# A GNN layer and an attention layer: SyncE fetches a chunk of every 7th block row by row, and ScalarE makes the node-side one-hot from broadcast rows

## The chip, the core and the metric

The kernel runs on one core of one Trainium2 chip. The metric is the device time of one execution in microseconds, median over several runs. The engines are TensorE (PE; PEld is its weight load), VectorE (DVE), ScalarE (ACT), GpSimd (POOL) and SyncE (SP). SyncE computes nothing here: it issues DMAs and waits on semaphores.

## The reference, cut to what matters

There are 12500 nodes with 128 features and 200000 edges sorted by `dst`. Layer normalisation and relu stand ahead of each of two layers; each layer's result is added to its input.

```python
h = relu(layernorm(x))
# layer 0: message passing, mlp(h) = silu(h @ W1 + b1) @ W2 + b2
msgs = mlp_msg(concat[mlp_node(h)[dst], mlp_node(h)[src], mlp_edge(edge_attr)])    # 200000 x 64
agg = segment_sum(msgs, dst) / max(count(dst), 1)
out = h + mlp_upd(concat[h, agg]);  x = x + layernorm(out) * ln_g + ln_b
# layer 1: graph attention, 4 heads of 32, with self loops
h = relu(layernorm(x)) @ W
e = leaky_relu(a_src[src] + a_dst[dst], 0.2)
p = exp(e - segment_max(e, dst)[dst])
out = segment_sum(h[src] * p / segment_sum(p, dst)[dst], dst)
return x + out + bias
```

## The kernel before, in words

**Tiling.** The edges form 196 blocks (`NB`) of 1024, each of 8 chunks (`C`) of 128 edges. The nodes form 98 windows (`W`) of 128. As the edges are sorted, a walk through (block, window) pairs takes 294 steps (`NS`), two to a row of the loop, 147 rows. `build_steps` in the message pass works out the step table on the chip: which block and window each step has, and (`blockend`) after which step a block is done with.

**Stages.** The opening (`opening`) does the layer normalisation and the node MLP and stores the source-side table `Btab`, 64 floats a node. Each of its weights comes by a load of its own (half of them issued by ScalarE, line 364), and VectorE folds small weights together ahead of the first group (lines 424 to 432). The message pass walks all steps; from row 100 on, its rows also carry the update phase (`update_mean` and so on), which makes the new x and the table `Htab`, 136 floats a node. The attention pass walks all steps again and gathers from `Htab`. Between two stages all engines meet at a barrier (line 832).

**Gathers.** GpSimd does little but gather: `gather_blocks` (line 529) issues one indirect DMA for each chunk, 128 rows by 128 indices (line 541), into the slot of its block; there are 7 slots (`SLOTS`), `p_rows` in the message pass and `a_G` in the attention pass. Ahead of a block it waits for that block's index list (`src`) and for the last step that uses the block whose slot it takes (`p_z`).

**Row fetches.** In every 14th block (`SPAN`) GpSimd leaves out the last chunk. SyncE fetches its 128 rows one by one over the 12 blocks before (class `Rows`): `load` brings the 128 node numbers, `batch` reads 12 or 8 of them into registers (line 580) and issues as many DMAs of one row (line 584) into a spare tile `p_single` or `a_single`, and `place` (line 597) copies the spare into the slot when the steps are done with it.

**SyncE's loop.** `feed_messages` (line 708) goes through the blocks in one order. For each it waits until edge attributes can be overwritten (`s_s1`), loads the edge attributes of the block 6 ahead (line 718), waits for its gathers (line 746), announces it (`s_ready`), loads the index list of the block that takes this slot next (line 714), and does its share of the row fetches. `feed_blocks` (line 621) is the same for the attention pass, with broadcast flag rows in place of edge attributes (line 1422). VectorE waits for `s_ready` in each step before it adds the gathered rows (line 1056).

**One-hots.** Each step needs two one-hot matrices between its 1024 edges and the 128 nodes of its window. VectorE makes one in bf16 with edges on the partitions: `dst` less the window's first node (`p_rel`, line 1078), compared with a ramp in PSUM (`p_Sb`, line 1089). ScalarE casts it to f32 as `p_S` (line 1227), the stationary side of the segment sum (line 1365). TensorE transposes its 8 chunks (line 1318) and ScalarE copies the result out of PSUM as `p_ST` (line 1206), nodes on the partitions, for the expansion of the target-side table (line 1346). Engines run each row's work in program order; semaphores count steps.

Of the kernel before, what the change touches and what calls it, by code (L numbers as in the profile page):

```python
# [21 lines left out]
I32 = mybir.dt.int32  # L22
ACT = mybir.ActivationFunctionType
AX = mybir.AxisListType

P = 128
# [6 lines left out]
C = 8  # L33
# [6 lines left out]
BATCH = (12, 12, 12, 8, 12, 8, 12, 8, 12, 8, 12, 12)  # L40
# [23 lines left out]
assert W == NG * GW and NG % 2 == 0 and NS % 2 == 0 and NB % SPAN == 0 and sum(BATCH) == P and len(BATCH) < SPAN  # L64
# [32 lines left out]
def build(nc, t, out):  # L97

    main = ExitStack()
    with main:  # L100
# [3 lines left out]
        x1keep = nc.dram_tensor("x1keep", [NP, D], F32, kind="Internal").ap()  # L104
        flagrows = nc.dram_tensor("flagrows", [NB, P], F32, kind="Internal").ap()

# [12 lines left out]
        for name, shape, dt in [  # L119
# [10 lines left out]
            ("xr", [P, W], F32), ("xs", [P, W], F32), ("flag", [P, NB], F32),  # L130
            ("nv", [P, WX, 3, 2 * NH], BF16), ("attn", [P, WX, 2 * NH], F32),
# [8 lines left out]

        k["at"] = sb("at", [1, P], I32)
        k["singles"] = [sem("at"), [sem(f"row{n}") for n in range(3)], sem("to")]
        k["slots"] = [[sem(f"{n}{u}") for u in range(SLOTS)] for n in ("src", "rows", "side")]

        k["idx"] = [sb(f"idx{u}", [P, C], I32) for u in range(SLOTS)]

        with ExitStack() as ctx:
            opening(nc, t, k, hTkeep, Btab, lambda *a: sb(*a, ctx=ctx), sem, ctx)
        with ExitStack() as ctx:
            message_pass(nc, t, k, Btab, Htab, hTkeep, x1keep, flagrows, lambda *a: sb(*a, ctx=ctx), sem, ctx)  # L150
        with ExitStack() as ctx:
            attention_pass(nc, t, k, Htab, flagrows, x1keep, out, lambda *a: sb(*a, ctx=ctx), sem, ctx)
# [61 lines left out]
def opening(nc, t, k, hTkeep, Btab, sb, sem, ctx):  # L214
# [13 lines left out]
    iota_i = sb("iota_i", [P, P * C], I32)  # L228
# [4 lines left out]
    s1 = sb("n_s1", [H, GW * P])  # L233
    psT, psU, psV = (ctx.enter_context(nc.psum_tensor(f"n_ps{n}", [P, 2, 512], F32)) for n in "TUV")
# [3 lines left out]
    s_w, s_wc, s_id, s_v, s_pe, s_zero = (sem(f"c_{n}") for n in ("w", "wc", "id", "v", "pe", "zero"))  # L238
# [23 lines left out]
    with nc.Block() as block:  # L262
        @block.sync
        def _(sp):
# [28 lines left out]
            run_pairs(sp, body, NG, 3)  # L293
            sp.wait_ge(s_wc, 32)
# [5 lines left out]
        def _(pool):  # L300
            pool.iota(iota_i[:, :], [[1, P], [0, C]], base=0, channel_multiplier=0).then_inc(s_id, 1)
            pool.memset(k["ident"][:, :], 0.0).then_inc(s_id, 1)
            pool.wait_ge(s_id, 2)
# [9 lines left out]
        def _(pe):  # L313
            pe.wait_ge(s_id, 3)
# [79 lines left out]
        def _(dve):  # L394
# [6 lines left out]
            def fold():  # L401
# [27 lines left out]
                dve.wait_ge(s_id, 3)  # L429
                dve.tensor_copy(k["iota_nc"][:, :, :].rearrange("p n c -> p (n c)"), iota_i[:, :]).then_inc(s_v, 1)  # L430
                dve.wait_ge(s_v, link())
                dve.tensor_copy(k["identb"][:, :], k["ident"][:, :]).then_inc(s_v, 1)
# [96 lines left out]
def gather_blocks(nc, pool, table, rows, idx, s_used, s_turn, k, turns, s_table=None):  # L529
# [3 lines left out]
    def block(i, odd, u, used):  # L533
        if due(16 * (i + 1 + turns)):
            pool.wait_ge(s_idx[u], 16 * (i + 1 + turns))
        if used is not None:
            if due(used):
                pool.wait_ge(s_used, used)
            pool.sem_inc(s_turn, 1)
        for c in range(C - 1 if odd and u == SLOTS - 1 else C):  # L540
            pool.indirect_dma_start(  # L541
                out=rows[:, u * C + c, :], out_offset=None, in_=table,
                in_offset=bass.IndirectOffsetOnAxis(ap=idx[u][:, c:c + 1], axis=0)).then_inc(s_g[u], 16)
# [5 lines left out]
    for u in range(SLOTS):  # L549
        block(0, False, u, None)  # L550
# [3 lines left out]
    for u in range(SLOTS):  # L554
        block(1, True, u, used[u])
    with pool.Fori(1, NB // SPAN) as r:
        used = used_by(r * SPAN, SPAN)
        for odd in range(2):
            for u in range(SLOTS):
                block(2 * r + odd, odd == 1, u, used[odd * SLOTS + u])  # L560


class Rows:


    def __init__(self, nc, sp, t, k, table, spare, at, to, s_used, s_turn, turn):
        self.nc, self.sp, self.t, self.k, self.table, self.spare, self.at, self.to = nc, sp, t, k, table, spare, at, to
        self.s_used, self.s_turn, self.turn = s_used, s_turn, turn
        self.s_at, self.s_row, self.s_to = k["singles"]
        self.total = NB // SPAN * turn  # L570

    def load(self, r):
        self.sp.dma_start(self.at[:, :], self.t["single"][bass.ds(r, 1), :]).then_inc(self.s_at, 16)

    def batch(self, r, n):
        sp, first = self.sp, sum(BATCH[:n])
        if n == 0:
            sp.wait_ge(self.s_at, 16 * (r + 1 + self.total))
            sp.sem_inc(self.s_turn, 1)
        which = self.nc.values_load_multi_w_load_instructions(  # L580
            self.at[0:1, first:first + BATCH[n]], engines=[sp.engine], min_val=0, max_val=NP - 1,
            skip_runtime_bounds_check_because="indices of nodes")[1]
# [4 lines left out]
    def place(self, r):  # L587
        sp = self.sp
        used = self.nc.values_load_multi_w_load_instructions(
            self.k["blockend"][0:1, 0, bass.ds(r * SPAN + SPAN - 1, 1)], engines=[sp.engine], min_val=0, max_val=NS,  # L590
            skip_runtime_bounds_check_because=BOUNDED)[1][0]
        for n in range(3):
            sp.wait_ge(self.s_row[n], 16 * sum(BATCH[n::3]) * (r + 1 + self.total))
            sp.sem_inc(self.s_turn, 1)
        sp.wait_ge(self.s_used, used)
        sp.sem_inc(self.s_turn, 1)
        sp.dma_start(self.to, self.spare[:, :]).then_inc(self.s_to, 16)

    def placed(self, r):
        self.sp.wait_ge(self.s_to, 16 * (r + 1 + self.total))  # L600
        self.sp.sem_inc(self.s_turn, 1)


def gathers(r, odd, u, turns):

    if u < SLOTS - 1:
        return 16 * C * (2 * r + odd + 1 + turns)
    return 16 * (2 * C - 1) * (r + turns // 2) + 16 * (2 * C - 1 if odd else C)


def step_singles(singles, r, n, final):

    if n < len(BATCH):
        singles.batch(r, n)
    elif n == SPAN - 2:
        singles.place(r)
    elif n == SPAN - 1 and not final:
        singles.load(r + 1)


def feed_blocks(nc, sp, t, idx, s_used, s_turn, s_ready, k, side, turns, then, singles):


    s_idx, s_g, s_side = k["slots"]

    def load_idx(b, u):
        sp.dma_start(idx[u][:, :], t["src"].rearrange("(b p) c -> b p c", p=P)[bass.ds(b, 1)]
                     .rearrange("o p c -> (o p) c")).then_inc(s_idx[u], 16)

    def arrived(r, odd, u):  # L630
        i = 2 * r + odd
        sp.wait_ge(s_g[u], gathers(r, odd, u, turns))
        sp.sem_inc(s_turn, 1)
        if due(16 * (i + 1 + turns)):
            sp.wait_ge(s_side[u], 16 * (i + 1 + turns))
# [4 lines left out]
    singles.load(0)  # L640
    then()
    def blocks(r, odd, first=False, final=False):
        i = 2 * r + odd
        used = used_at(i)
        for u in range(SLOTS):
            if odd and u == SLOTS - 1:
                singles.placed(r)
            arrived(r, odd, u)
            if not final:
# [1226 lines left out]
```

## Time and profile before

| | |
|---|---|
| median of 3 runs | 4092.73 us (4090.88 to 4094.87) |
| the profiled execution | 4091.22 us, span 4089.1 us, mean granted clock 0.838 |
| busy of the span | PE 83%, PEld 73%, DVE 62%, ACT 70%, POOL 73% |
| gathers | 1554 in each pass, 1471.4 us busy in the message pass, 1470.8 in the attention pass |
| first gather, message pass / attention pass | 112.13 us / 2109.75 us |

How to read the rows further down: times are microseconds from the span's start, a mean is in ns. A row names line, engine, operation, and out<-in by the program's names, without buffer numbers. "SPq" and "POOLq" are the queues in which SyncE and GpSimd issue. "issue" is time in which an engine waited for nothing that the profile shows. The share of busy time is an average over stages with different limits; the views by stage say more.

### The profile page before, as it was taken

To read this page: it belongs to the slowest core of one execution; us is meant where nothing else is said; L and a number is where in the kernel's file an instruction comes from. 1 tells how busy PE (TensorE), PEld (TensorE's weight loads), DVE (VectorE), ACT (ScalarE), POOL (GpSimd) and SP (SyncE) were. 2 spreads that over 40 slices of the span, in tenths; PEclk is the share of its full clock that TensorE was granted. 3 is DMA by queue.
4 is the path that set the end of the run, shared out by engine and by line. 5 is a ranking of instruction groups with operands and counts; after the bars stand their busy time and mean duration, and the time that the engine had idled before them with its cause. 6 is when DMAs were issued, how large, how long until landed. Compare 5 with 4: busy or idle time off the path is not lost. (4 is left out here: it accounts for less than half of the span.)

```text
span 4089.1 us, 126775 instructions
## 1 busy us (share of the span) xinstructions
PE 3382.9 (83%) x30848; PEld 2976.2 (73%) x30849; DVE 2517.0 (62%) x10511; ACT 2850.5 (70%) x5940; POOL 2965.8 (73%) x3134
## 2 busy tenths in 40 slices
PE   7789888999988899999947777777777778777777
PEld 4677777777777788888847777777777767766776
DVE  5752222222222256777748777777777777888888
ACT  6466565656556577788738777777777777877777
POOL 2677777777777777777737777777777777777774
PEclk8789999999899899999967777777777777777777
DMA  5322222222222233333342222222222222332332
GB/s 159 88 60 53 54 55 53 56 53 53 55 54 53 60 83 91 91 96 95 81 120 58 57 58 58 57 58 58 58 57 58 58 58 63 79 78 76 78 78 58
DMA packets 319769, 282.90 MB, mean 69 GB/s; under 512 B 143418, under 2 KB 242924, under 8 KB 319532
## 3 DMA queue, kind: packets, MB, share of 16 engines
q0 software_dynamic: 99456, 159.33, 15.9%
q1 hardware_dynamic: 139224, 79.62, 7.4%
q10 hardware_dynamic: 80852, 41.75, 3.5%
q14 instruction: 205, 1.68, 0.1%
q8 instruction: 32, 0.52, 0.1%
HBM read 249.58 MB, written 29.40 MB: 68 GB/s over the span
## 5 line engine op out<-in xcount | busy, mean ns | idle before, releaser
L541 POOL DMA_INDIRECT a_G<-Htab,idx x1554 | 1470.8, 946 | 526.3 <-issue 464.0
L541 POOL DMA_INDIRECT p_rows<-Btab,idx x1554 | 1471.4, 947 | 475.1 <-issue 473.4
L1799 PE MATMUL a_psA<-a_GP,a_S 128*128 128x132 f32 x4704 | 892.5, 365 | 2.7 <-DVE a_GP L1634 2.7
L1799 PEld LDWEIGHTS a_psA<-a_GP,a_S 128*128 128x128 f32 x4704 | 821.5, 268 | 8.2 <-DVE a_GP L1634 3.1
L1056 DVE TENSOR_TENSOR p_z<-p_psZ,p_rows 128x512 f32<-128x512 f32 x294 | 195.9, 689 | 829.4 <-SPq L746 679.6
L1206 ACT COPY p_ST<-p_psT 128x1024 bf16<-128x1024 bf16 x294 | 300.5, 1022 | 563.7 <-PE p_psT L1318 543.4
L1730 ACT CAST a_S<-a_Sb 128x512 f32<-128x512 bf16 x588 | 608.6, 1144 | 0.0
L1365 PE MATMUL p_psA<-p_msg,p_S 128*128 128x65 f32 x4704 | 589.9, 284 | 10.9 <-ACT p_S L1227 9.8
L1365 PEld LDWEIGHTS p_psA<-p_msg,p_S 128*128 128x128 f32 x4704 | 571.6, 201 | 16.5 <-issue 12.8
L1227 ACT CAST p_S<-p_Sb 128x1024 f32 (+1 forms) x294 | 582.6, 1982 | 0.0
L1341 PEld LDWEIGHTS p_psZ<-wc,p_s 128*128 128x128 f32 x2352 | 325.1, 206 | 204.7 <-issue 103.5
L1341 PE MATMUL p_psZ<-wc,p_s 128*128 128x128 f32 x2352 | 339.3, 291 | 80.0 <-DVE p_z L1056 80.0
L1324 PE MATMUL p_psH<-arena,ew 128*128 x588 | 350.3, 680 | 24.1 <-issue 0.2
L1634 DVE TENSOR_TENSOR a_GP<-a_G,a_ep 128x1056 f32<-128x1056 f32 x294 | 366.8, 1248 | 0.0
L1688 ACT COPY a_ST<-a_psT 128x1024 bf16<-128x1024 bf16 x294 | 302.6, 1029 | 45.0 <-issue 27.4
L1318 PE MATMUL p_psT<-identb,p_Sb 128*128 128x128 bf16 x2352 | 292.8, 260 | 44.3 <-issue 25.1
L1318 PEld LDWEIGHTS p_psT<-identb,p_Sb 128*128 (+1 forms) x2352 | 255.6, 147 | 82.5 <-issue 62.5
L1705 ACT ACTIVATE arena<-arena,a_f x1176 | 282.3, 311 | 7.1 <-DVE arena L1516 1.7
L1789 PE MATMUL a_psCD<-ident,a_csh 4*128 4x4 f32 x588 | 140.6, 307 | 158.6 <-DVE a_csh L1522 157.1
L1789 PEld LDWEIGHTS a_psCD<-ident,a_csh 4*128 4x128 f32 x588 | 114.8, 242 | 207.2 <-DVE a_csh L1522 202.9
L1346 PE MATMUL p_psZ<-arena,p_ST 128*128 x7056 | 264.4, 196 | 0.0
L1346 PEld LDWEIGHTS p_psZ<-arena,p_ST 128*128 128x128 bf16 x7056 | 258.1, 100 | 4.7
(212 smaller groups left out, 5165.8 us busy)
## 6 DMA issues: line engine op xcount, KB each, us to landing
arena<-in_ea SPq DMA_DIRECT2D x196, 256.0 KB
p_single<-Btab SPq DMA_DIRECT2D x1792, 0.2 KB
a_single<-Htab SPq DMA_DIRECT2D x1792, 0.5 KB
p_rows<-Btab,idx POOLq DMA_INDIRECT x1554
a_G<-Htab,idx POOLq DMA_INDIRECT x1554
Htab<-u_H ACTq DMA_DIRECT2D x49, 136.0 KB
arena<-Htab SPq DMA_DIRECT2D x7, 952.0 KB
n_x<-in_x SPq DMA_DIRECT2D x14, 448.0 KB, 4.0
```

The lines of the kernel that those rows point to most:

```text
L541: pool.indirect_dma_start(out=rows[:, u * C + c, :], out_offset=None, in_=table, in_offset=bass.IndirectOffsetOnAxis(ap=idx[u][:, c:c + 1] ...
L1206: act.copy(ST[u][:, :, :], psT[:, :, :]).then_inc(s_ST, 1)
L1227: act.copy(S32[v][:, :, :].rearrange("p c n -> p n c"), onehot(row - 3 + u, v)).then_inc(s_S32, 1)
L1318: m = pe.transpose(psT[:, c, :], hot[:, :, c], k["identb"][:, :])
L1324: pe.matmul(psH[:, :], k["ew1"][:, :], ea[:, bass.ds(slot, 1), :].rearrange("p o e -> p (o e)"), start=True, stop=True).then_inc(s_H, 1)
L1341: pe.matmul(psZ[v][:, 2 * e:2 * e + 2, :], s1[v][:, e * P:(e + 1) * P], k["wc2"][:, :], start=e == 0, stop=False)
L1346: m = pe.matmul(psZ[v][:, c, :], ST[v][:, c, :], a, start=False, stop=part == 2 and c == C - 1)
L1365: m = pe.matmul(psA[v], S32[v][:, c, :], msg[v][:, c, :], start=c == 0, stop=c == C - 1)
L1634: dve.tensor_tensor(GP[u][:, :, :].rearrange("p c (h f) -> p c h f", h=NH), G[:, slot2, 0:HR].rearrange("p c (h f) -> p c h f", h=NH), bc( ...
L1688: act.copy(ST[v][:, :, :], psT[:, :, :]).then_inc(s["ST"], 1)
L1730: m = act.copy(S32[v][:, cs, :].rearrange("p c n -> p n c"), Sb[v][:, :, cs])
L1799: m = pe.matmul(psA[v][:, 0:HR], S32[v][:, c, :], GP[v][:, c, :], start=c == 0, stop=c == C - 1)
```

## The change

**Row fetches.** The row-wise chunk is now that of every 7th block: the last chunk of the last block in each round of 7, save in the first round, so 27 rounds a pass instead of 14. SyncE spreads the 128 rows over 7 blocks (19, 18, 18, 18, 18, 18, 19). The node numbers are multiplied by the row's size once, in the opening, and stored in DRAM (`offsets`); `batch` reads byte offsets and addresses the table as a flat array of bytes. The spare and the offsets are double-buffered. One index list holds a whole round, 128x56, and is loaded once in 7 blocks.

**One-hots of the message pass.** For each block SyncE loads one more thing, `load_near`: the block's 1024 targets modulo 128, in bf16, one row of DRAM (`lowrows`, made in the opening) broadcast to 128 partitions. ScalarE makes `p_ST` from it in two passes, `Abs` of the row less the partition's number and `Relu` of one less that. The transposes, their PSUM tile and the copy go. VectorE writes the f32 one-hot `S32` itself, one instruction from the ramp in PSUM, `wnode` and `dst`; the bf16 one-hot and ScalarE's cast go. `psH` has two buffers.

**The opening** loads `nodes` and `ends` (the targets as 98 rows), masks and casts the latter to `low`, multiplies the former twice, and SyncE stores `offsets` and `lowrows` at its end, with a wait for each.

```diff
-BATCH = (12, 12, 12, 8, 12, 8, 12, 8, 12, 8, 12, 12)
+BATCH = (19, 18, 18, 18, 18, 18, 19)
...
             run_pairs(sp, body, NG, 3)
+            sp.wait_ge(s_off, 18)
+            for n in range(2):
+                sp.dma_start(offsets[n], bytes_[n][:, :]).then_inc(s_off, 16)
+            sp.wait_ge(s_off, 50)
+            sp.wait_ge(s_low, 18)
+            sp.dma_start(lowrows.rearrange("(q r) e -> q (r e)", r=2), low[:, :]).then_inc(s_low, 16)
+            sp.wait_ge(s_low, 34)
...
             for to, src in loads[1::2]:
                 act.dma_start(to, src).then_inc(s_w, 16)
+            act.dma_start(nodes[:, :], t["single"]).then_inc(s_off, 16)
+            act.dma_start(ends[:, :], t["dstrow"].rearrange("(q r) e -> q (r e)", r=2)).then_inc(s_low, 16)
...
+                dve.tensor_scalar(k["back"][:, :], row_i[:, :], -1.0, None, ALU.mult).then_inc(s_v, 1)
...
+                dve.tensor_scalar(ends[:, :], ends[:, :], P - 1, None, ALU.bitwise_and).then_inc(s_low, 1)
+                dve.wait_ge(s_low, 17)
+                dve.tensor_copy(low[:, :], ends[:, :]).then_inc(s_low, 1)
...
-    def block(i, odd, u, used):
-        if due(16 * (i + 1 + turns)):
-            pool.wait_ge(s_idx[u], 16 * (i + 1 + turns))
+    def block(r, odd, u, used, whole=False):
+        if u == 0:
+            pool.wait_ge(s_idx[odd], 16 * (r + 1 + turns // 2))
...
-        for c in range(C - 1 if odd and u == SLOTS - 1 else C):
+        for c in range(C if whole or u < SLOTS - 1 else C - 1):
...
-        which = self.nc.values_load_multi_w_load_instructions(
-            self.at[0:1, first:first + BATCH[n]], engines=[sp.engine], min_val=0, max_val=NP - 1,
+        at = self.nc.values_load_multi_w_load_instructions(
+            self.k["at"][0:1, odd * P + first:odd * P + first + BATCH[n]], engines=[sp.engine], min_val=0,
...
-            sp.dma_start(self.spare[first + p:first + p + 1, :], self.table[bass.ds(which[p], 1), :]
-                         ).then_inc(self.s_row[n % 3], 16)
+            sp.dma_start(self.spare[first + p:first + p + 1, odd, :].bitcast(U8),
+                         self.table[bass.ds(at[p], self.size)].unsqueeze(0)).then_inc(self.s_row[n % 4], 16)
...
+    def step(self, i, odd, u, first, final):
+        if not first and u == 0:
+            self.landed(i)
+        if not first and u == SLOTS - 2:
+            self.place(i, odd)
+        if not final:
+            self.batch(i + 1, 1 - odd, u)
+            if u == 0 and not (isinstance(i, int) and i + 2 >= ROUNDS):
+                self.load(i + 2, odd)
...
+    def load_near(b, u):
+        sp.dma_start(near[:, u, :], lowrows[bass.ds(b, 1), :].rearrange("o e -> (o e)").partition_broadcast(P)
+                     ).then_inc(s_ea[u], 16)
...
+                        dve.scalar_tensor_tensor(
+                            S32[v][:, :, :], bc(psI[:, :], 1, C), k["wnode"][:, bass.ds(j, 1)],
+                            bc(k["dstf"][:, bass.ds(blk[u], 1), :].rearrange("p o c -> p (o c)"), 2, P),
+                            ALU.subtract, ALU.is_equal).then_inc(s_S32, 1)
...
-                        act.copy(ST[u][:, :, :], psT[:, :, :]).then_inc(s_ST, 1)
+                        act.activation(ST[u][:, :, :].rearrange("p c n -> p (c n)"), dist[:, :], ACT.Relu,
+                                       scale=-1.0, bias=k["one"][:, :]).then_inc(s_ST, 1)
...
-                        act.copy(S32[v][:, :, :].rearrange("p c n -> p n c"), onehot(row - 3 + u, v)).then_inc(s_S32, 1)
...
-                        for c in range(C):
-                            m = pe.transpose(psT[:, c, :], hot[:, :, c], k["identb"][:, :])
-                        m.then_inc(s_T, 1)
```

On SyncE, in the message pass, one block of the loop stood like this (line 584 goes on in the same pairs for 12 or 8 rows):

```order
L718 DMA arena<-in_ea 128x512
L714 DMA idx0<-in_src 128x8
L580 TENSOR_LOAD at
L584 ISA
L584 DMA p_single<-Btab 1x64
L584 ISA
L584 DMA p_single<-Btab 1x64
```

Now one block stands like this:

```order
L749 DMA arena<-in_ea 128x512
L752 DMA p_S32<-lowrows 128x1024
L612 TENSOR_LOAD at
L616 DMA p_single<-Btab 1x256 x18
```

The instruction ahead of each row (the register work that the profile records as FUSED_REGOPS) and the index list of each block are gone; the broadcast rows (`p_S32` is the tile of which `near` is a part) are new.

On GpSimd, the message pass, where the second round ends and the loop begins, with the semaphores waited for, before:

```order
L541 DMA p_rows<-Btab,idx5 128x64 [waits src5,p_z]
L541 DMA p_rows<-Btab,idx5 128x64 x7
L541 DMA p_rows<-Btab,idx6 128x64 [waits src6,p_z]
L541 DMA p_rows<-Btab,idx6 128x64 x6
...
L541 DMA p_rows<-Btab,idx0 128x64 [waits src0,p_z]
```

The last two blocks of a loop's first round and the first of its second, now:

```order
L571 DMA p_rows<-Btab,idx0 128x64 [waits p_z]
L571 DMA p_rows<-Btab,idx0 128x64 x7
L571 DMA p_rows<-Btab,idx0 128x64 [waits p_z]
L571 DMA p_rows<-Btab,idx0 128x64 x6
L571 DMA p_rows<-Btab,idx1 128x64 [waits src1,p_z]
L571 DMA p_rows<-Btab,idx1 128x64 x7
```

The wait for an index list stands once in 7 blocks instead of at each, and every round's last block has 7 gathers where every second one had.

On SyncE, from the opening's last store to the message pass, before:

```order
L283 DMA Btab<-n_b1 128x7x64
L262 UNCONDITIONAL_BRANCH
L833 UNCONDITIONAL_BRANCH
L714 DMA idx0<-in_src 128x8
```

And now:

```order
L291 DMA Btab<-n_b1 128x7x64
L304 DMA offsets<-bytes0 28x128
L304 DMA offsets<-bytes1 28x128
L307 DMA lowrows<-low 98x2048
L270 UNCONDITIONAL_BRANCH
L868 UNCONDITIONAL_BRANCH
L657 DMA idx0<-in_src 128x56
```

Three stores moved in between the table's last rows and the end of the stage, and one index list of 56 columns stands where seven of 8 stood.

## Rows read from the trace of the kernel before

**Rows 1.** The page's part 4: the chain that ended last, by engine, by line.
```profile
POOL 27%; issue 11%; DVE 4%; PE 3%; DMA 1%; DVEq 1%; POOLq 1%; ACT 0%; SPq 0%; ACTq 0%
POOL a_G L541 27%; PE a_psA L1799 2%; DMA a_G<-Htab,idx 1%; DVE a_GP L1634 1%; POOLq L546 0%; DVE a_csh L1522 0%; DVE arena L1516 0%; DVEq L1409 0%; PE a_psCD L1789 0%; PE a_psCD L1834 0%; DVE nv L83 0%; DVE a_e L1527 0%; DVE a_loc L1461 0%; DVE a_nq L1554 0%; DVE a_eq L1539 0%
```

**Rows 2.** The page's part 5: count | busy us, mean ns | idle before, its releaser.
```profile
L541 POOL DMA_INDIRECT a_G<-Htab,idx x1554 | 1470.8, 946 | 526.3 <-issue 464.0
L541 POOL DMA_INDIRECT p_rows<-Btab,idx x1554 | 1471.4, 947 | 475.1 <-issue 473.4
```

**Rows 3.** Timeline of GpSimd: start, length, instruction, [idle before]; first, last, first gather.
```profile
112.13 1.17 POOL L541 DMA_INDIRECT p_rows<-Btab,idx  x1 [1.66 <-DMA idx<-in_src]
...
2056.02 0.94 POOL L541 DMA_INDIRECT p_rows<-Btab,idx  x1 [0.30 <-issue]
...
2109.75 0.94 POOL L541 DMA_INDIRECT a_G<-Htab,idx  x1 [52.79 <-POOLq L832]
```

**Rows 4.** Timelines of SyncE, VectorE and GpSimd: block 60 and its slot's refill.
```profile
720.00 0.36 SPq L714 DMA_DIRECT2D idx<-in_src  x1
720.20 1.29 DVE L1056 TENSOR_TENSOR p_z<-p_psZ,p_rows 128x512 f32<-128x512 f32 x2 [5.32 <-SPq L746]
778.59 0.94 POOL L541 DMA_INDIRECT p_rows<-Btab,idx  x1 [0.30 <-issue]
```

**Rows 5.** What SyncE's queue waited for: total us, times, longest.
```profile
SPq L746 <- DMA p_rows<-Btab,idx: 644.2, 194, 7.0
SPq L633 <- DMA a_G<-Htab,idx: 569.9, 168, 6.9
```

**Rows 6.** Timelines of ScalarE, VectorE and SyncE: the opening, and two stage starts.
```profile
8.47 0.55 ACTq L364 DMA_DIRECT2D attd<-in_att_dst  x1
...
20.84 0.69 DVE L430 CAST iota_nc<-iota_i 128x1024 bf16<-128x1024 int32 x1
...
102.12 5.08 SPq L283 DMA_DIRECT2D Btab<-n_b  x2
109.76 3.50 SPq L714 DMA_DIRECT2D idx<-in_src  x7
...
2109.08 2.32 SPq L1422 DMA_DIRECT2D a_frow<-flagrows  x7
```

**Rows 7.** Timeline of SyncE: two blocks of the message pass.
```profile
700.36 0.36 SPq L714 DMA_DIRECT2D idx<-in_src  x1
701.86 4.83 SPq L584 DMA_DIRECT2D p_single<-Btab  x12
...
710.46 0.36 SPq L714 DMA_DIRECT2D idx<-in_src  x1
711.76 3.19 SPq L584 DMA_DIRECT2D p_single<-Btab  x8
```

**Rows 8.** Instructions of line 584: count, ns min/median/max, first and last start.
```profile
L584 SPq FUSED_REGOPS  x3584: 37/37/47, 126.7 to 4042.8; - x200
L584 SPq MOVE p_single<-Btab x1792: 29/29/38, 126.8 to 2045.6; - x200
L584 SPq DMA_DIRECT2D p_single<-Btab x1792: 224/228/308, 126.9 to 2045.7; - x200
```

**Rows 9.** Windows: us, busy of PE, PEld, DVE, ACT, POOL, PEclk, DMA share, GB/s.
```profile
1600.00:1800.00 200.00, 194.65 (x1967) 165.05 (x1963) 139.61 (x564) 158.91 (x267) 151.20 (x161) 0.99 0.36 95
2200.00:2600.00 400.00, 306.64 (x2608) 283.42 (x2606) 311.28 (x1452) 302.82 (x850) 302.44 (x321) 0.74 0.23 58
```

**Rows 10.** The message pass's wide groups; the last from 300 to 1300 us alone.
```profile
L1056 DVE TENSOR_TENSOR p_z<-p_psZ,p_rows 128x512 f32<-128x512 f32 x294 | 195.9, 689 | 829.4 <-SPq L746 679.6
L1206 ACT COPY p_ST<-p_psT 128x1024 bf16<-128x1024 bf16 x294 | 300.5, 1022 | 563.7 <-PE p_psT L1318 543.4
L1227 ACT CAST p_S<-p_Sb 128x1024 f32 (+1 forms) x294 | 582.6, 1982 | 0.0
L1318 PE MATMUL p_psT<-identb,p_Sb 128*128 128x128 bf16 x2352 | 292.8, 260 | 44.3 <-issue 25.1
...
L1089 DVE TENSOR_TENSOR p_Sb<-p_psI,p_rel 128x1024 bf16 x151 | 97.3, 686 | 7.0 <-DVE p_rel L1078 3.0
```

More of the change, by code:

```diff
@@ L22 @@
 I32 = mybir.dt.int32
+U8 = mybir.dt.uint8
 ACT = mybir.ActivationFunctionType
@@ L130, in build @@
             ("xr", [P, W], F32), ("xs", [P, W], F32), ("flag", [P, NB], F32),
+            ("back", [P, 1], F32), ("one", [P, 1], F32),
             ("nv", [P, WX, 3, 2 * NH], BF16), ("attn", [P, WX, 2 * NH], F32),
@@ L554, in gather_blocks @@
     for u in range(SLOTS):
-        block(1, True, u, used[u])
-    with pool.Fori(1, NB // SPAN) as r:
+        block(0, 1, u, used[u])
+    with pool.Fori(1, ROUNDS // 2) as r:
         used = used_by(r * SPAN, SPAN)
@@ L569, in __init__, with load, batch @@
         self.s_at, self.s_row, self.s_to = k["singles"]
[L570 to L575, printed above, removed]
+        self.before = (ROUNDS - 1) * turn
+    def load(self, i, odd):
+        self.sp.dma_start(self.k["at"][0:1, odd * P:(odd + 1) * P], self.offsets[bass.ds(i, 1), :]).then_inc(self.s_at, 16)
+    def batch(self, i, odd, n):
         sp, first = self.sp, sum(BATCH[:n])
@@ L601, in placed @@
+    def placed(self, i):
+        self.sp.wait_ge(self.s_to, 16 * (i + self.before))
         self.sp.sem_inc(self.s_turn, 1)
-def gathers(r, odd, u, turns):
-    if u < SLOTS - 1:
[L607 to L618, printed above, removed]
@@ L621, in feed_blocks, with landed @@
[L621 to L632, printed above, removed]
+    def landed(self, i):
+        for n in range(4):
+            self.sp.wait_ge(self.s_row[n], 16 * sum(BATCH[n::4]) * (i + self.before))
+            self.sp.sem_inc(self.s_turn, 1)
@@ L639, in feed_blocks @@
         side(u, u)
-    singles.load(0)
+    singles.load(1, 1)
     then()
@@ L655, in blocks @@
                 side(i * SLOTS + u + 2, (u + 2) % SLOTS)
-            step_singles(singles, r, odd * SLOTS + u, final)
+            singles.step(i, odd, u, first, final)
     def used_at(i):
@@ L739, in blocks @@
                 load_ea(i * SLOTS + u + SLOTS - 1, ahead)
+                load_near(i * SLOTS + u + SLOTS - 1, ahead)
             if not (final and u > 1):
-                sp.wait_ge(s_ea[landing], 16 * (i + 1 + (u > 1)))
+                sp.wait_ge(s_ea[landing], 32 * (i + 1 + (u > 1)))
                 sp.sem_inc(s_eardy, 1)
-            if odd and u == SLOTS - 1:
-                singles.placed(r)
-            sp.wait_ge(s_g[u], gathers(r, odd, u, 0))
+            if u == SLOTS - 1 and not first:
+                singles.placed(i)
+            sp.wait_ge(s_g[u], gathers(i, u, 0))
             sp.sem_inc(s_ready, 1)
-            load_idx(u if final else (i + 1) * SLOTS + u, u)
-            step_singles(singles, r, odd * SLOTS + u, final)
+            if u == 0:
+                load_idx(sp, t, k, 0 if final else i + 1, 1 - odd)
+            singles.step(i, odd, u, first, final)
     def used_at(i):
@@ L1302, in body @@
                     m.then_inc(s_ft, 1)
+                if isinstance(row, int) and 1 <= row <= NG:
+                    pe.wait_ge(s_piece, PIECE * row)
                 if isinstance(row, int) and row == HIDE:
```

215 lines of the change are left out of this document (112 added, 103 removed).

## Prediction

> **What bounds the kernel now.** I read the chain that ended last first, then the two costliest groups. The chain is one long run of GpSimd gathers with "issue" between them [rows 1]. Each pass has 1554 of them, 0.947 us busy and 0.304 us of issue apiece [rows 2]: (1471.4 + 473.4) / 1554 = 1.251 us from one gather to the next. Nearly all idle time before them is "issue", so GpSimd waits for nobody: in the message pass 473.4 of 475.1 us. The two passes are 2 x 1945 of 4089 us; what is left is the opening (first gather at 112.13), the 53 us between the last gather of pass one and the first of pass two [rows 3], and a tail of a few steps. Whatever the change does to VectorE, ScalarE and TensorE counts only if one of them, or SyncE, becomes slower than the gathers.
>
> How far is that? In the message pass SyncE announces block 60 just ahead of its next index list at 720.00, VectorE adds the rows at 720.20, and GpSimd refills that slot at 778.59 [rows 4]: the consumers could be over 50 us later before a gather waits. SyncE is the engine to watch. It idles on landing gathers for 644.2 us of the message pass and 569.9 us of the attention pass [rows 5], which is 46.0 and 40.7 us in each stretch of 14 blocks, 111 x 1.251 = 138.9 us long.
>
> **1. Fewer gathers: a gain.** Before, GpSimd drops one gather in 14 blocks; now it drops one in 7, except in the first round: 56 + 27 x 55 = 1541 instead of 1554. That is 13 x 1.251 = 16.3 us a pass, -32.5 us in both, as long as GpSimd stays the bound. One wait per block on the index list becomes one per 7 blocks; that is worth nothing, since the wait doesn't show between gathers.
>
> **2. The opening: a loss.** ScalarE issues two more loads (0.55 us each [rows 6]) ahead of its first activation, which the first group waits for: +1.1. VectorE's fold gets a mask over 98x2048 int32, a cast of that to bf16 and four small operations. The nearest row is a 128x1024 int32 to bf16 cast of 0.69 us [rows 6]; so the cast is 1.4, the mask 1.4 to 2.8 (I take 2.0), the small ones 4 x 0.25: +4.4. The groups behind run as a dependent chain, so I let both shift the end. Then SyncE, before it closes the opening, stores the offsets, waits, stores the masked rows, waits. Now it goes from the end of its last issue (102.12 + 5.08 = 107.20) to the next stage at 109.76 [rows 6], 2.56 us with one landing in it. Two stores in sequence are two such landings with some 1.5 us of issues, and the old wait lies under the first: +4.0. Sum **+9.5 us**, bounds +5 (mask cheap, part of the chain slack) and +14.
>
> **3. SyncE's work: the term that decides.** In 14 blocks of the message pass it is busy 138.9 - 46.0 = 92.9 us now. Per 14 blocks the change does this:
> - Rows: 256 instead of 128. Now one costs (4.83 - 3.19) / 4 = 0.41 us [rows 7]: FUSED_REGOPS 37, MOVE 29 and the DMA 228 ns [rows 8], so 0.116 us of gaps, 0.039 each. The new row has its byte offset ready, and the register instruction is gone from the order above: 0.41 - 0.037 - 0.039 = 0.334. Ends: 0.30 (the remaining instructions with one gap) and 0.41 (nothing saved). Back-to-back issues without any register instruction between them took 2.32 / 7 = 0.33 [rows 6], so it can't be much less; I take 0.34, as the first rows of a batch are longer. 256 x 0.34 - 128 x 0.41 = +34.6.
> - Register loads: between an index issue's end and the first row lie 1.14 us for 12 values and 0.94 for 8 [rows 7], 0.05 per value, so 1.45 for 18: 14 x 1.45 - 12.9 = +7.4.
> - Index lists: 12 of 14 issues go (0.36 and two register instructions, 0.5): -6.0.
> - The broadcast rows: one more 128-partition issue per block, 0.55: +7.7.
> - A second set of waits, list load and placing store: +2.
>
> Sum 92.9 + 45.7 = **138.6 us against 110 x 1.251 = 137.6 for the gathers**. This is a tie. SyncE would fall behind by 1.0 us in 14 blocks, 13 us over the 13.5 stretches in which it fetches rows, and it starts some 4 us later, since the first broadcast rows wait for the step table. The last round has no rows to fetch, so SyncE catches up there; the steps (10.5 in it, at 6.55 us) catch up only as far as engines allow. TensorE is busy 194.65 of 200 us late in the pass [rows 9], 6.4 us a step, and loses 1.0 us of transposes [rows 10]: at about 5.5 us a step 10 us are made up. Of a 17 us backlog 7 are left; I take **+5**, ends 0 and 75 (below).
> In the attention pass the same changes without the broadcast rows give 138.9 - 40.7 + 38.0 = 136.2 against 137.6. GpSimd stays the bound there, by 1.4 us in 14 blocks: **0**.
>
> **4. The one-hots: nothing.** ScalarE loses the 1.98 us cast and the 1.02 us copy and gets two 128x1024 activations; the copy of that size is the nearest row [rows 10], so 2 x 1.02: -0.96 us a step. VectorE trades the 0.69 us bf16 one-hot for a 128x1024 f32 one; the nearest row is 128x512 f32 out of PSUM in 0.69 [rows 10], 1.4 at twice the size: about +0.7 a step, on an engine at 139.61 of 200 us [rows 9]. TensorE loses 8 transposes. All lie beside gathers with 50 us of slack. After the last gather ScalarE's casts go and VectorE's one-hots come in a few rows, -3 to +3.
>
> What VectorE does could reach GpSimd in one way. Late in the message pass, with VectorE at 70%, GpSimd is busy 151.20 of 200 us, and 302.44 of 400 in the attention pass with VectorE at 78% [rows 9]: the same 75.6%, so nothing on VectorE slows it today. The Trainium skill ("SBUF — State Buffer", Who interferes with whom) says that a VectorE instruction with two SBUF inputs, or in a two-port mode, keeps GpSimd out of a shared port, and that one with at most one SBUF input doesn't. The new one-hot takes its ramp from PSUM and its indices from SBUF; by the rule it costs nothing, as in my sum.
>
> **The sum.** 4091.2 (profiled execution, span 4089.1) - 32.5 + 9.5 + 5 = 4073.2. The median of the runs is 1.5 above that execution: **4075**.
>
> **Rivals.**
> - *SyncE becomes the bound of the message pass* (slower). If a row doesn't shrink as worked out, or an issue stretches when issues stand closer, each 0.01 us adds 2.6 us to 14 blocks, 35 us to the pass. The point: 4101 needs a backlog of about 41 us, (41 - 4) / 13.5 = 2.7 over the gathers, a row of 0.347. At 0.36: 143.7, 6.1 x 13.5 = 82 + 4 - 10 = 76, so about 4145; at the old 0.41 some 4315, and the attention pass would bind too. For it: the margin is zero. Against: the order has one instruction less in each row, and its time is in the rows.
> - *The gain of pass one is given back*: the same with a row of 0.341 to 0.347, a backlog of 24 to 40 us: 4084 to 4101, no measurable change.
> - *More gain*: SyncE stays ahead (row 0.33 or less) and the fold hides: -32.5 + 5, so 4060 to 4064.
> - *TensorE's clock* falls once the transposes are gone. It shows 0.99 with TensorE at 97% late in the message pass and 0.74 at 77% in the attention pass, between its two levels of 1.2 and 2.4 GHz [rows 9]. At 0.74, 5.4 us of steps would take 7.2, over the 6.55 of the gathers: 0.65 x 94 (the steps from row 100 on, where the update work runs) = 60, less what is absorbed, about 4120. But then TensorE would never idle, and the row with no idle time shows 0.99. The Trainium skill ("TensorE: Matmul & The Clock Gate", HAM oscillation) makes idle gaps the cause of the lower level; by that rule this rival limits itself.
> - *The port*: were GpSimd held for each new one-hot, 294 x 1.4 = up to 412 us, about 4485. Only the rows above speak, and they speak against it.
>
> **How the numbers follow.** A measurement of this kernel can tell about 0.2% (8.2 us) from no change: faster is under 4084.5, slower over 4100.9. Forecast, 4062 to 4084: 0.51. More gain: 0.06. Given back: 0.17. SyncE the bound: 0.20. Clock: 0.04. Port: 0.02. So faster 0.57, same 0.17, slower 0.26. Below 4062 I leave 0.06; above 4125 half of the SyncE case and the port, 0.12: the range is 4062 to 4125; the forecast's own is 4062 to 4084.
>
> **What the next profile shows.** 1541 gathers a pass, still 1.25 us apart, with "issue" before them. Row fetches 0.33 to 0.35 us apart without FUSED_REGOPS. SyncE's idle time on landing gathers nearly gone in the message pass (under 100 us, from 644) and some 20 to 60 us in the attention pass. First gather at about 121 instead of 112, first attention gather at 2102 or so, the end 20 us earlier. I am wrong if GpSimd waits on VectorE's sums in the message pass, if a row takes over 0.347 us, or if the opening grows by more than 14 us.

## The result: slower by 15%, and the profile after

The changed kernel takes 4721.77 us (median of 4 runs, 4715.08 to 4730.44) against 4091.81 before: a ratio of 1.154, 95% interval 1.152 to 1.156. The forecast was 4075, the range 4062 to 4125. The profiled execution has a span of 4719.1 us at a mean granted clock of 0.76 (0.838 before).

The page of the changed kernel, part 4, the chain that ended last, by engine and by line, against [rows 1]:

```profile
SPq 38%; issue 8%; DVE 1%; DVEq 0%; PE 0%; ACT 0%; ACTq 0%
SPq L616 19%; SPq L612 15%; SPq L1449 1%; SPq L694 1%; SPq L1454 0%; SPq L657 0%; SPq L626 0%; SPq L621 0%; PE a_psA L1826 0%; SPq L605 0%; DVEq L1436 0%; DVE arena L1543 0%; DVE a_csh L1549 0%; SPq L671 0%; SPq L668 0%
```

The chain is SyncE's. Line 616 is the row DMA; line 612 is the instruction that loads a list of byte offsets into SyncE's registers. GpSimd is no longer among the engines on the chain. The chain reaches back to the start of the attention pass; for the message pass the waits further down speak. Part 5 of the same page, the gathers against [rows 2], and VectorE's add of the gathered rows against [rows 10]:

```profile
L571 POOL DMA_INDIRECT a_G<-Htab,idx x1541 | 1458.6, 947 | 817.8 <-issue 461.5
L571 POOL DMA_INDIRECT p_rows<-Btab,idx x1541 | 1458.2, 946 | 811.8 <-issue 444.9
L1091 DVE TENSOR_TENSOR p_z<-p_psZ,p_rows 128x512 f32<-128x512 f32 x294 | 196.9, 688 | 1220.4 <-SPq L783 1112.8
```

13 gathers a pass are gone and one still takes 0.946 us, but GpSimd now idles 812 us before them where it idled 475. VectorE waits 1112.8 us for SyncE's announcement that a block is there (line 783), and GpSimd in turn for VectorE and, in the message pass, for index lists that SyncE loads late. The waits of GpSimd and of SyncE in the changed kernel (what was waited for: us in total, times, longest; line 867 is the barrier between stages), SyncE's against [rows 5]:

```profile
POOL p_rows L571 <- DVE p_z L1091: 302.5, 72, 13.0
POOL a_G L571 <- DVE a_GP L1661: 260.2, 117, 12.7
POOL a_G L571 <- POOLq L867: 96.1, 1, 96.1
...
POOL p_rows L571 <- DMA idx<-in_src: 64.4, 14, 9.0
...
SPq L668 <- DMA a_G<-Htab,idx: 5.7, 1, 5.7
...
SPq L783 <- DMA p_rows<-Btab,idx: 3.1, 1, 3.1
```

SyncE hardly waits for gathers any more: 3.1 us in the message pass, from 644.2, and 5.7 in the attention pass, from 569.9. The pace follows from the windows (us, busy of PE, PEld, DVE, ACT, POOL with counts, PEclk, DMA share, GB/s), one in the middle of each pass:

```profile
600.00:2000.00 1400.00, 997.16 (x9046) 840.38 (x9045) 468.67 (x1042) 650.32 (x861) 863.69 (x915) 0.81 0.27 74
2800.00:4400.00 1600.00, 1109.05 (x9056) 1027.52 (x9056) 1112.73 (x5189) 1051.60 (x2953) 1049.32 (x1111) 0.69 0.21 55
```

915 gathers in 1400 us make 110 x 1400 / 915 = 168.3 us for 14 blocks of the message pass, 1111 in 1600 us make 158.4 in the attention pass. GpSimd alone would need 137.6, and the prediction's sum for SyncE was 138.6 and 136.2.

Where the 630 us of the span went is read from the first and the last gather of each pass, against [rows 3]:

```profile
115.55 1.18 POOL L571 DMA_INDIRECT p_rows<-Btab,idx  x1 [2.02 <-DMA idx<-in_src]
...
2382.55 0.94 POOL L571 DMA_INDIRECT p_rows<-Btab,idx  x1 [0.30 <-issue]
...
2479.62 0.94 POOL L571 DMA_INDIRECT a_G<-Htab,idx  x1 [96.12 <-POOLq L867]
...
4658.95 0.94 POOL L571 DMA_INDIRECT a_G<-Htab,idx  x1 [0.30 <-issue]
```

The first gather comes at 115.55, 3.4 later; the message pass's gathers take 2268.0 us, 323 more; from the last of them to the first of the attention pass it is 96.1 us, 43 more; the attention pass's gathers take 2180.3, 236 more; the tail after the last gather is 24 longer, 59 us from 35.

### The profile page after: what moved, and what is told of

Its sections match the earlier page's. It is cut to its first block and busy times, and to the rows that moved or that the text cites. A ratio compares the mean times of both kernels' runs of the same rounds, so it can differ in the third digit from the quotient of the medians.

```text
span 4719.1 us, 122417 instructions
## 1 busy us (share of the span) xinstructions
PE 3338.5 (71%) x28496; PEld 2919.1 (62%) x28497; DVE 2625.8 (56%) x10223; ACT 2691.3 (57%) x5940; POOL 2940.4 (62%) x3109
## 5 line engine op out<-in xcount | busy, mean ns | idle before, releaser
L1091 DVE TENSOR_TENSOR p_z<-p_psZ,p_rows 128x512 f32<-128x512 f32 x294 | 196.9, 688 | 1220.4 <-SPq L783 1112.8
L1368 PEld LDWEIGHTS p_psZ<-wc,p_s 128*128 128x128 f32 x2352 | 378.5, 239 | 596.3 <-DVE p_z L1091 486.8
L1368 PE MATMUL p_psZ<-wc,p_s 128*128 128x128 f32 x2352 | 408.0, 329 | 441.3 <-DVE p_z L1091 441.1
L1245 ACT ACTIVATE p_s<-p_psH,eb 128x512 f32<-128x512 f32 x294 | 199.7, 679 | 467.3 <-PE p_psH L1351 467.2
L1241 ACT ACTIVATE p_ST<-p_dist,one 128x1024 bf16<-128x1024 bf16 x294 | 337.5, 1148 | 105.6 <-PE p_psZ L1373 90.8
L1260 ACT ACTIVATE p_msg<-p_z 128x512 f32<-128x512 f32 x294 | 185.8, 632 | 359.1 <-DVE p_z L1091 358.6
L1235 ACT ACTIVATE p_dist<-p_S,back 128x1024 bf16 x294 | 335.8, 1142 | 90.8 <-issue 57.4
L1861 PE MATMUL a_psCD<-ident,a_loc 128*4 128x128 f32 x294 | 95.2, 324 | 411.2 <-DVE a_loc L1488 363.2
L1698 ACT COPY a_ca<-a_G 128x32 f32 x294 | 72.7, 247 | 524.7 <-SPq L671 516.7
L1109 DVE SCALAR_TENSOR_TENSOR p_S<-p_psI,wnode,dstf 128x1024 f32<-128x1024 f32 x294 | 364.1, 1280 | 0.0
L1488 DVE TENSOR_TENSOR_SCAN a_loc<-scanmask,a_ca 128x32 f32<-128x32 f32 x294 | 66.4, 226 | 461.4 <-ACT a_ca L1698 451.2
```

The costliest lines, as they stand in the source:

```text
L1109: dve.scalar_tensor_tensor(S32[v][:, :, :], bc(psI[:, :], 1, C), k["wnode"][:, bass.ds(j, 1)], bc(k["dstf"][:, bass.ds(blk[u], 1), :].rear ...
L1235: act.activation(dist[:, :], near[:, bass.ds(blk1[u] % SLOTS, 1), :].rearrange("p o e -> p (o e)"), ACT.Abs, bias=k["back"][:, :]).then_in ...
L1241: act.activation(ST[u][:, :, :].rearrange("p c n -> p (c n)"), dist[:, :], ACT.Relu, scale=-1.0, bias=k["one"][:, :]).then_inc(s_ST, 1)
L1368: pe.matmul(psZ[v][:, 2 * e:2 * e + 2, :], s1[v][:, e * P:(e + 1) * P], k["wc2"][:, :], start=e == 0, stop=False)
```

## What SyncE does in a block

The timeline of SyncE in the changed kernel, two blocks of the message pass, against [rows 7] (start, length, instruction; line 657 is the index list, 616 the row fetches, 749 the edge attributes, 752 the broadcast rows):

```profile
708.76 0.33 SPq L657 DMA_DIRECT2D idx<-in_src  x1
711.45 6.58 SPq L616 DMA_DIRECT2D p_single<-Btab  x19
...
718.72 0.36 SPq L749 DMA_DIRECT2D arena<-in_ea  x1
719.27 0.36 SPq L752 DMA_DIRECT2D p_S<-lowrows  x1
723.75 5.79 SPq L616 DMA_DIRECT2D p_single<-Btab  x18
729.80 0.36 SPq L749 DMA_DIRECT2D arena<-in_ea  x1
```

The rows are what they were worked out to be: 5.79 / 18 = 0.32 us each, 0.33 on average over the pass. But from 719.63, the end of the broadcast load's issue, to 723.75 nothing is issued, 4.1 us, where the prediction had 1.45. The instructions of line 612, first the two of these blocks and then all of them (count, ns min/median/max, first and last start):

```profile
L612 SPq TENSOR_LOAD <-at x1: 1613/1613/1613, 709.7 to 709.7; - x1
...
L612 SPq TENSOR_LOAD <-at x1: 3844/3844/3844, 719.8 to 719.8; - x1
...
L612 SPq TENSOR_LOAD <-at x378: 1603/3852/4593, 134.6 to 4619.7; - x189
```

The first load of a round, 19 values, takes 1.61 us; the next, 18 values, 3.84. Over the seven loads of a round the medians in the message pass are 1.61, 3.85, 3.84, 3.85, 3.84, 3.71 and 4.04 us. The trace of the kernel before has such loads too, 8 or 12 values (line 580) and 7 values of the table of block ends (line 751):

```profile
L580 SPq TENSOR_LOAD <-at x336: 528/942/1292, 125.9 to 4037.1; - x168
...
L751 SPq TENSOR_LOAD <-blockend x28: 1108/1643/1918, 121.0 to 1996.2; - x28
```

Seven values took 1.64 us there where twelve took 0.94. The lists of line 580 start at 0, 12, 24, 36, 44 and so on, all multiples of 4; the changed kernel's at 0, 19, 37, 55, 73, 91, 109. The table of line 751 is the third row of 203 values in its tile, so its lists start at 406, 413, 420, 427 and so on. Every fourth of them starts at a multiple of 4, and these seven took 1.11 to 1.13 us, the 21 others at least 1.64. The third and the fourth:

```profile
L751 SPq TENSOR_LOAD <-blockend x1: 1120/1120/1120, 255.0 to 255.0; - x1
...
L751 SPq TENSOR_LOAD <-blockend x1: 1643/1643/1643, 331.0 to 331.0; - x1
```

## Experiments

**Theory A**: a load goes four values at a time where its list starts at a multiple of 4 values, and one by one elsewhere. **Theory B**: the loads are slow because of the row fetches in flight ahead of them. **Theory C**: they are slow because they are long.

**Batches of 20 and 16.** Every list starts at a multiple of 4.

```diff
-BATCH = (19, 18, 18, 18, 18, 18, 19)
+BATCH = (20, 20, 16, 20, 16, 20, 16)
```

> The changed kernel with batches of 20, 20, 16, 20, 16, 20, 16 rows, so that each list of register values starts at a multiple of 4 values. Theory A (SyncE's register load reads four values at a time only where its list starts at a multiple of 4 values, and one by one elsewhere, 0.21 us each): a load of 16 or 20 takes 1.1 to 1.5 us instead of 3.85, SyncE's work for 14 blocks falls from 168 to about 136 us, under the 137.6 of the gathers; GpSimd is the bound again, and the time is 4062 to 4080 us. Theory B (the loads are slow because they stand behind row fetches that are still in flight, the first of a round being fast because it follows a wait): loads after the first stay at 3.8 us or more, the time stays at about 4720. Theory C (a load of more than some 16 values is slow): the loads of 16 are fast, those of 20 are not, the time is about 4450.

Measured: 4079.23 us, a ratio of 0.9965 to the kernel before (0.9952 to 0.9977). All loads of line 612, and SyncE's waits:

```profile
L612 SPq TENSOR_LOAD <-at x378: 1131/1251/1904, 142.8 to 3975.7; - x189
...
SPq L668 <- DMA a_G<-Htab,idx: 170.7, 72, 9.9
SPq L783 <- DMA p_rows<-Btab,idx: 95.9, 26, 10.1
```

Another list of batch sizes takes 640 us off, and GpSimd is the bound again: its gathers take 1927.2 and 1930.2 us in the two passes, from 1944.8 and 1944.3 in the kernel before. Theories B and C fall: behind as many row fetches as before, loads of 16 take 1.13 us and loads of 20 take 1.36.

**Batches of 18.** Every other list starts at a multiple of 4, the others at a multiple of 2.

```diff
-BATCH = (19, 18, 18, 18, 18, 18, 19)
+BATCH = (18, 18, 18, 18, 18, 18, 20)
```

> The changed kernel with batches of 18, 18, 18, 18, 18, 18, 20 rows: the lists start at 0, 18, 36, 54, 72, 90, 108, so every other one is at a multiple of 4 values and the others at a multiple of 2 alone, with the same rows in flight ahead of each. Theory A: loads 3, 5 and 7 of a round take 1.4 to 1.6 us, loads 2, 4 and 6 either stay at 3.85 (four at a time needs a multiple of 4) or fall to about 2.3 (pairs); the time is then about 4350 or about 4150. Theory B: all six stay at 3.8, time about 4720.

Measured: 4323.04 us (one run). Three loads in a row, lists at 18, 36 and 54, all of 18 values behind 18 row fetches:

```profile
L612 SPq TENSOR_LOAD <-at x1: 3835/3835/3835, 897.9 to 897.9; - x1
...
L612 SPq TENSOR_LOAD <-at x1: 1561/1561/1561, 909.1 to 909.1; - x1
...
L612 SPq TENSOR_LOAD <-at x1: 3855/3855/3855, 918.4 to 918.4; - x1
```

The same count in the same surroundings takes 1.56 or 3.84 us by its start alone, and a multiple of 2 is no better than an odd start.

**The kernel before, its lists one value off.**

```diff
-BATCH = (12, 12, 12, 8, 12, 8, 12, 8, 12, 8, 12, 12)
+BATCH = (11, 12, 12, 8, 12, 8, 12, 8, 12, 8, 12, 13)
```

> The kernel before with batches of 11, 12, 12, 8, 12, 8, 12, 8, 12, 8, 12, 13: every list after the first starts one value short of a multiple of 4. Theory A: 12 values take 2.6 us instead of 0.94 and 8 take 1.7 instead of 0.72, 16 us more for SyncE in 14 blocks, which its 46 us of idle time take up: its waits on landing gathers fall from 644 to about 420 us in the message pass, and the time stays within 5 us of the kernel before. Theories B and C: the loads stay at 0.94 and 0.72, since their surroundings and counts are the same.

Measured: 4092.41 us, a ratio of 1.0009 (1.0000 to 1.0019). The loads of line 580, and SyncE's waits:

```profile
L580 SPq TENSOR_LOAD <-at x336: 1158/2662/3142, 122.6 to 4043.8; - x168
...
SPq L746 <- DMA p_rows<-Btab,idx: 395.4, 178, 7.2
SPq L633 <- DMA a_G<-Htab,idx: 315.2, 127, 6.9
```

Twelve values take 2.66 us and eight 1.86. SyncE loses some 250 us of idle time in each pass and the time doesn't move: the same price is free where SyncE has 46 us to spare in 14 blocks. From all loads of these kernels: off a multiple of 4, 1.86 us for 8 values, 2.66 for 12, 3.84 for 18 and 4.04 for 19, which is 0.20 us a value and some 0.25 at the start; at a multiple of 4, 0.72 for 8, 0.94 for 12, 1.13 for 16 and 1.36 for 20, which is some 0.21 for each four values. The Trainium skill ("Runtime: NRT & Kernel Launch", Instruction fetch mechanics) has about 200 ns a register even for loads in bulk; the runs, whose lists lie in SBUF, agree for lists off a multiple of 4 and differ for those on it.

**The two parts apart.** The row fetches alone are the kernel before with the changed `Rows`, `gather_blocks` and index lists, and batches of 20 and 16. Against the run with these batches:

```diff
-            sp.dma_start(lowrows.rearrange("(q r) e -> q (r e)", r=2), low[:, :]).then_inc(s_low, 16)
...
-                load_near(i * SLOTS + u + SLOTS - 1, ahead)
...
-                        dve.scalar_tensor_tensor(
-                            S32[v][:, :, :], bc(psI[:, :], 1, C), k["wnode"][:, bass.ds(j, 1)],
...
+                        dve.tensor_tensor(onehot(row, u), psI[:, :, :], bc(rel[u][:, :], 1, P),
+                                          ALU.is_equal).then_inc(s_S, 1)
...
+                            m = pe.transpose(psT[:, c, :], hot[:, :, c], k["identb"][:, :])
```

The one-hots alone are the kernel before with these same lines the other way round, the new one-hots in and the row fetches, index lists and opening stores of offsets as they were:

```diff
+                load_near(i * SLOTS + u + SLOTS - 1, ahead)
...
+                        dve.scalar_tensor_tensor(
+                            S32[v][:, :, :], bc(psI[:, :], 1, C), k["wnode"][:, bass.ds(j, 1)],
...
-                            m = pe.transpose(psT[:, c, :], hot[:, :, c], k["identb"][:, :])
```

> The row fetches alone: byte offsets, every 7th block, batches of 20 and 16 as in the run before, but the one-hots, the transposes and the opening's masks of the kernel before. Theory A (GpSimd binds both passes, so each gather left out is worth 1.25 us, and the new one-hots bring nothing but their cost: 8 us in the opening and about 7 us more between the last gather of the message pass and the first of the attention pass): 4092 - 32.5 + 4 for the offsets in the opening = 4063 us, with the stretch between the passes back at 53 us from 60.6 and SyncE's idle time on landing gathers in the message pass at about 200 us, 108 more than with the broadcast rows. Rival D (the one-hots carry part of the gain, by giving TensorE time): the time is 4079 us or more, and GpSimd waits for VectorE's sums in the update rows.

> The one-hots alone, with the row fetches of the kernel before (every 14th block, batches of 12 and 8). Theory A: 1554 gathers a pass at 1.251 us as before; the opening is some 8 us longer and the stretch between the passes about 7 us longer, so about 4105 us (4098 to 4112); SyncE's idle time on landing gathers in the message pass falls from 644 to about 530 us. Rival D: 4092 us or less.

In this comparison every kernel took 6700 to 6900 us, the kernel before too (6938.79), with VectorE and ScalarE waiting for what the profile calls remote (row fetches 6919.67, ratio 0.9971; one-hots 6692.39, ratio 0.9639). Why is open, and so is why the one-hots gained there. Both were run again. The expectation speaks of another chip; the record has the same number, 13, for both comparisons, and in the second the kernel before took 4091.89 us.

> The row fetches alone once more, on another chip: in the run above every kernel of the comparison, the kernel before too, took some 6900 us. Theory A as there: 4092 - 32.5 + 4 = 4063 us, the stretch between the passes at 53 us, SyncE's idle time on landing gathers in the message pass at about 200 us. Rival D: 4079 us or more.

> The one-hots alone once more, on another chip. Theory A as above: about 4105 us (4098 to 4112), 1554 gathers a pass 1.251 us apart, SyncE's idle time on landing gathers in the message pass at about 530 us. Rival D: 4092 us or less. On the chip of the run above the one-hots alone took 3.6% off all the same, where TensorE, VectorE and ScalarE waited for what the profile calls remote and GpSimd waited for VectorE; if the gain came from there being fewer instructions, nothing of it shows here.

Measured: the row fetches alone 4066.11 us, ratio 0.9936 (0.9922 to 0.9951); the one-hots alone 4095.05, ratio 1.0012 (1.0003 to 1.0020). SyncE's wait on gathers in the message pass and the first gather of the attention pass (in brackets GpSimd's idle time before it, the stretch between the passes), first of the row fetches, then of the one-hots:

```profile
SPq L762 <- DMA p_rows<-Btab,idx: 226.8, 94, 10.1
...
2105.26 0.94 POOL L557 DMA_INDIRECT a_G<-Htab,idx  x1 [61.11 <-POOLq L849]
```

```profile
SPq L769 <- DMA p_rows<-Btab,idx: 533.0, 174, 6.7
...
2114.86 0.94 POOL L557 DMA_INDIRECT a_G<-Htab,idx  x1 [53.62 <-POOLq L852]
```

The gain is the row fetches'; the one-hots alone cost about 3 us and 111 us of SyncE's idle time (644.2 to 533.0), 0.57 us a block, where the prediction gave the broadcast load 0.55. Two expectations fell. The longer stretch between the passes is there with the old one-hots (61.1 us) and not with the new ones alone (53.6, from 52.8). And the one-hots alone were expected at 4098 to 4112 and came out below that: the stretch did not grow by 7, and the first gather came 4.3 us later, not 8.

**Batches levelled.** Fewer rows in the block that has the index list and in the one that places.

```diff
-BATCH = (20, 20, 16, 20, 16, 20, 16)
+BATCH = (16, 20, 20, 20, 20, 16, 16)
```

> The row fetches alone with batches of 16, 20, 20, 20, 20, 16, 16: fewer rows in the block that also has the index list, the waits on landed rows and the table of block ends, and fewer where the spare is placed. With 20, 20, 16, 20, 16, 20, 16 SyncE announced the seven blocks of a round 3.7, 4.1, 3.0, 1.6, 1.6, 1.9, 3.2 us after their last gather, before 1.4 to 1.9. Theory E (the 7 to 8 us by which the stretch between the passes grew, 61 from 53, are these late announcements, which the update rows can't win back since TensorE is busy 97% there): the announcements come 2 us or less behind in most blocks, the stretch goes back to 53 to 56 us, and the time falls by about 5, to 4061. Rival F (the stretch is set by something else, as the kernel before with slower register loads showed 60 us there with announcements on time): it stays near 60 and the time at 4066.

> The whole change with batches of 16, 20, 20, 20, 20, 16, 16. With 20, 20, 16, 20, 16, 20, 16 the announcements came 6.7, 7.8, 7.1, 5.2, 4.5, 2.7, 5.0 us behind in the message pass. Theory E: 3 to 6 us behind, the stretch between the passes 2 to 4 us shorter than 60.6, the time 4074 to 4078. Rival F: no change of the stretch, 4079.

Measured: the row fetches alone 4064.68 us, ratio 0.9932 (0.9919 to 0.9946); the whole change 4067.48, ratio 0.9946 (0.9933 to 0.9960). These two and the row fetches above can't be told from one another; all three are 0.5 to 0.7% faster than the kernel before. The first gather of the attention pass, row fetches alone and whole change:

```profile
2102.04 0.94 POOL L557 DMA_INDIRECT a_G<-Htab,idx  x1 [63.46 <-POOLq L849]
```

```profile
2099.02 0.94 POOL L571 DMA_INDIRECT a_G<-Htab,idx  x1 [57.20 <-POOLq L867]
```

The announcements came 1.5 to 2.4 us (row fetches alone) and 2.0 to 3.5 us (whole change; medians by block of a round) behind the last gather, as levelling meant. With the row fetches alone the stretch stayed long all the same, as rival F has it; with the whole change it became 3 us shorter, as theory E has it. But its time fell by 12 us, below the 4074 to 4078 expected: of the 14.1 us between the two profiled spans 8.7 lie in the opening, whose first 100 us had a granted clock of 0.97 here and of 0.85 with batches of 20 and 16. The windows from 1700 to 2000 us, of the first and of the second, say what differs there:

```profile
1700.00:2000.00 300.00, 293.14 (x2952) 249.05 (x2947) 208.97 (x844) 239.55 (x402) 227.10 (x240) 0.99 0.34 93
```

```profile
1700.00:2000.00 300.00, 270.42 (x2642) 217.96 (x2639) 231.38 (x825) 227.13 (x411) 226.84 (x241) 0.99 0.44 121
```

With the transposes TensorE is busy 98% of these update rows, without them 90%. That a TensorE with nothing to spare can't follow gathers that end sooner, so that what GpSimd gains in these rows comes back behind the last gather, fits these rows; it is argued and not shown, since the kernel before with its lists one value off had 60.2 us there with no gather taken away:

```profile
2114.78 0.94 POOL L541 DMA_INDIRECT a_G<-Htab,idx  x1 [60.20 <-POOLq L832]
```

Each of these stretches is from one profiled execution; what sets them stays open.

## Why the prediction was wrong, by its own steps

- **The bound and the slack** were read rightly: GpSimd bound both passes, and SyncE was the engine to watch.
- **Fewer gathers (-32.5)**: right in size where GpSimd binds. With batches of 20 and 16 the two runs of gathers are 17.6 and 14.1 us shorter, 31.7 together. In the changed kernel they were gone as well, and worth nothing.
- **SyncE's row (0.334, taken as 0.34)**: right, 0.33 on average over each pass; line 616 has no FUSED_REGOPS, as the order showed.
- **SyncE's register loads (+7.4)**: the step that failed. From 12 values at 1.14 us and 8 at 0.94 it made 0.05 us a value and 1.45 for 18. Both rows were of lists that start at a multiple of 4; of the new lists only the first does, and their loads took 2 x (1.61 + 3.85 + 3.84 + 3.85 + 3.84 + 3.71 + 4.04) = 49.5 us in 14 blocks, with 0.2 us of gaps each 52.3, against the 14 x 1.45 = 20.3 of the sum. 138.6 + 32.0 = 170.6, measured 168.3. The rows that spoke against it, seven values in 1.64 us from most starts and in 1.12 from every fourth, were in the trace of before and were not used. The term was also given no bounds of its own, while the row's price had them to 0.01 us.
- **The tie** (138.6 against 137.6): nearly right. With cheap loads SyncE's waits on gathers were, from 300 to 1800 us and from 2300 to 3800 us, where every round fetches rows:

```profile
SPq L783 <- DMA p_rows<-Btab,idx: 31.0, 12, 3.2
```

```profile
SPq L668 <- DMA a_G<-Htab,idx: 101.8, 52, 3.3
```

That is 2.8 and 9.3 us in 14 blocks, so SyncE's work was about 135 and 128 against the 138.6 and 136.2 of the sum: 4 and 8 us too high, in which terms is not told apart. (Of the 95.9 us of the whole message pass 57.0 lie behind 1950 us, where the last round fetches no rows.) The loads of the changed kernel cost 32 us more in 14 blocks than those of this run, so its work should be 167 and 161, and its pace was 168.3 and 158.4: the loads account for the loss to within 3 us.
- **The opening (+9.5)**: the first gather came 3.4 us later in the changed kernel, 3.3 in the levelled one, 12.0 with batches of 20 and 16. But the granted clock of the first 100 us was 0.88 in the kernel before, 0.97 in the first two and 0.85 in the third. The kernel before with its lists one value off has the same opening as the kernel before and had 0.95 there; its first gather came at 108.23, 3.9 earlier:

```profile
108.23 1.17 POOL L541 DMA_INDIRECT p_rows<-Btab,idx  x1 [1.26 <-DMA idx<-in_src]
```

Against that run the changed kernel's came 7.3 us later. At granted clocks that are close, then, the opening costs 7 to 12 us, and +9.5 was a fair value; the 3.4 alone would mislead. The parts are there: the third group's statistics start at 27.59 instead of 22.12 (5.5, as summed), and from the end of the last table store's issue to the next stage it is 6.2 us instead of 2.6 (3.6 for 4.0). The groups behind the fold make up nearly half of the 5.5: the last group's statistics start at 90.43 instead of 87.48.
- **What the steps make up at the end of pass one (+5)**: the prediction had SyncE end the pass with a backlog, of which the steps win 10 us back. With batches of 20 and 16 there was none to speak of: the announcements of the last round came 1.5 to 3.4 us behind their gathers. The stretch between the passes still grew, from 52.8 to 60.6 us, for a cause that is open. That the sum had +5 near this place is luck.
- **The one-hots (0)**: right. VectorE's takes 1.28 us (1.4 estimated), ScalarE's two 1.14 and 1.15 (1.02 each). Alone they cost 0.12%; on top of the row fetches 3 us with levelled batches (4067.48 against 4064.68) and 13 with batches of 20 and 16 (4079.23 against 4066.11, from two comparisons), of which 10 lie in the opening.
- **TensorE's clock**: this rival did not come true. With batches of 20 and 16 the granted clock from 1600 to 1800 us was 0.98, near the level of 2.4 GHz, with TensorE busy 176.02 of 200 us, and GpSimd's gathers waited for "issue" alone.
- **The port**: gathers took 0.946 us beside the new one-hots and 0.947 before. The Trainium skill's rule ("SBUF — State Buffer", Who interferes with whom) gave no cost here, and the trace shows none.
- **The rival that came true** is the first, SyncE as the bound. It was given 0.20 and was priced by the row's length alone, at most 4315; its cause was another instruction of the same engine. With the loads at their measured price, 14 blocks at 168.3 and 158.4 us instead of 137.6 are 30.7 x 13.5 = 414 and 20.8 x 13.5 = 281 us. The consumers' slack is used up first, and comes back as the longer stretches behind each pass, 43 and 24 us; that leaves 371 and 257, against 340 and 252 measured over the 1927.8 us that 1541 gathers need.

With the lists on multiples of 4 the change comes out near the forecast of 4075: 4079 us and, levelled, 4067. The terms that carried the forecast, the gathers and the opening, are there; that the total is so close is in part luck, since the stretch between the passes stands in for the backlog that did not come.

## What to carry to other kernels

When an engine that issues DMAs is near its limit, price every instruction of its loop from rows, the register loads with the row fetches, and give each its own bounds; an extrapolation over a count holds only while everything else about the instruction, its start address too, stays as in the rows that it rests on. Look for a row of the same instruction elsewhere in the trace that contradicts the slope before using it. And cut lists that are read into registers at multiples of four values: here that alone was worth 640 us.

## What was not expected of the hardware

A register load on SyncE depends on where its list starts: 18 values took 3.84 us from a start at 18 or 54 and 1.56 from a start at 36. GpSimd's loads do the same: its lists of 14 values (line 546 of the kernel before) took 1.29 us from a multiple of 4 and 3.16 elsewhere. Off a multiple of 4 every value costs its 0.20 us: 18 values took 3.85 us from a start at 19 and as much from one at 18. These loads are not counted as busy in the profile, so that SyncE's limit shows only as an absence of waits and as its lines on the chain.
